# Mixer and feed-forward kernel: diagonals and loads of x placed in other slices of the opening

## The reference

```
low = x
for two levels:
    l = dwconv(low, h_filter)[:, ::2];  h = dwconv(low, g_filter)[:, ::2]     # 4 taps per channel, stride 2
    highs.append(h);  low = l
low = linear_attention(low, 16 heads)          # q = k = elu(x)+1, v = x, kv summed over the whole sequence
for the two levels, backwards:
    low = dwconv(repeat2(low), h_synth) + dwconv(repeat2(h), g_synth)
a = layer_norm(x + low, gamma, beta)
x1 = layernorm(x + a)
y = (silu(x1 @ wg.T) * (x1 @ wu.T)) @ wd.T     # 1536 hidden, integer weights times 1/127
out = layernorm(x1 + y)
```

## Time and profile before

| | us |
|---|---|
| median of 3 runs | 1210.11 |
| lowest and highest of them | 1209.3, 1210.5 |
| the profiled execution, its own time | 1209.61 |
| its span, from the first to the last instruction | 1207.8 |
| TensorE busy in the span | 1173.7 (97%) |
| VectorE busy | 973.1 (81%) |
| ScalarE busy | 672.6 (56%) |
| POOL busy | 303.1 (25%) |

### The profile page before, as it was taken

One profiled execution on the slowest core, in us unless ns is written; L12 is line 12 of the kernel. 1 busy time (PEld: TensorE's weight loads), 2 busy tenths in 40 slices (PEclk: granted clock), 3 DMA queues, 4 the chain that ended last, 5 costly groups with the idle time before them and its releaser, 6 DMA issues.

```text
span 1207.8 us, 19489 instructions
## 1 busy us (share of the span) xinstructions
PE 1173.7 (97%) x6456; PEld 604.4 (50%) x6456; DVE 973.1 (81%) x1951; ACT 672.6 (56%) x1403; POOL 303.1 (25%) x730
## 2 busy tenths in 40 slices
PE   6888999999999999999999999999999999999997
PEld 5567644445445544445445444444445444454443
DVE  7797999998999989997997779867997689845331
ACT  6954744677346854576346644666346644565342
POOL 0014322152314313152213412142304313131101
PEclk9998999999999999999999999999999999999999
DMA  7886520222212310222102310211111310110000
GB/s 263 271 201 142 184 61 19 106 97 89 71 44 79 128 40 18 98 83 74 36 27 97 98 35 18 105 62 53 35 58 64 106 35 11 42 55 1 3 34 35
DMA packets 52301, 92.96 MB, mean 77 GB/s; under 512 B 9072, under 2 KB 28784, under 8 KB 51312
## 3 DMA queue, kind: packets, MB, share of 16 engines
q1 hardware_dynamic: 50480, 87.10, 21.9%
q0 software_dynamic: 1728, 4.72, 2.2%
HBM read 67.09 MB, written 25.19 MB: 76 GB/s over the span
## 4 chain that ended last, share of the span: by engine, by line
PE 81%; DVE 6%; ACT 5%; issue 4%; POOL 3%; DMA 1%; SPq 0%; POOLq 0%; ACTq 0%; DVEq 0%
PE ps_up L679 12%; PE ps_up L680 12%; PE ps_gate L679 12%; PE ps_gate L680 12%; PE ps_down L698 12%; PE ps_down L697 12%; PE ps_x L622 2%; PE ps_y L640 2%; DVE l L1286 1%; PE ps_x L601 1%; POOL rs L1216 1%; PE ps_down L864 1%; DVE h L1286 1%; ACT x_hi L1136 1%; DVE hid L1286 1%
## 5 line engine op out<-in xcount | busy, mean ns | idle before, releaser
L697 PE MATMUL ps_down<-w,hid 128*128 128x512 f16 x768 | 291.4, 379 | 1.2 <-DVE hid L1672 1.0
L698 PE MATMUL ps_down<-w,hid 128*128 128x512 f16 x768 | 291.3, 379 | 0.0
L679 PE MATMUL ps_up<-x_hi,w 128*128 128x512 f16 x760 | 288.4, 379 | 0.9 <-DVE h_f L1685 0.9
L679 PE MATMUL ps_gate<-x_hi,w 128*128 128x512 f16 x760 | 288.4, 379 | 0.5 <-ACT h_f L1160 0.5
L680 PE MATMUL ps_gate<-x_lo,w 128*128 128x512 f16 x760 | 288.3, 379 | 0.0
L680 PE MATMUL ps_up<-x_lo,w 128*128 128x512 f16 x760 | 288.2, 379 | 0.0
L1160 ACT ACTIVATE h_f<-ps_gate 128x512 f32<-128x512 f32 x192 | 113.9, 593 | 205.6 <-PE ps_gate L680 204.6
L1685 DVE SCALAR_TENSOR_TENSOR h_f<-ps_up,h_f 128x512 f32<-128x512 f32 x192 | 130.9, 685 | 110.1 <-PE ps_up L680 97.7
L1152 ACT ACTIVATE hid<-h_f 128x512 f16<-128x512 f32 x192 | 119.7, 623 | 42.0 <-DVE h_f L1685 42.0
L1672 DVE TENSOR_TENSOR hid<-h_f,hid 128x512 f16<-128x512 f32 x192 | 130.9, 682 | 1.9 <-ACT hid L1152 1.0
L679 PEld LDWEIGHTS ps_up<-x_hi,w 128*128 128x128 f16 x760 | 74.2, 98 | 91.5 <-DVE h_f L1685 1.8
(11 more groups left out here) (260 smaller groups left out, 1688.0 us busy)
## 6 DMA issues: line engine op xcount, KB each, us to landing
xt<-x_tok SPq DMA_DIRECT2D x64, 256.0 KB, 2.7
out<-x SPq DMA_DIRECT2D x64, 256.0 KB, 2.0
xb<-x_chan SPq DMA_DIRECT2D x7, 2060.0 KB, 7.7
xa<-x_chan SPq DMA_DIRECT2D x20, 515.0 KB, 5.0
w<-weights POOLq DMA_DIRECT2D x12, 384.0 KB, 9.9
att<-den SPq DMA_DIRECT2D x32, 129.5 KB, 2.7
xa<-x_phase SPq DMA_DIRECT2D x8, 515.0 KB, 6.4
q_in<-q_scratch SPq DMA_DIRECT2D x7, 518.0 KB, 4.5
```

What stands on the lines that cost most here:

```text
L679: pe.matmul(ps_gu[k % 2][g][:, :], w, x1_hi[:, b, c, :], start=(c == 0), stop=False)
L697: pe.matmul(ps_d[t % 2][:, :], h_hi[:, k, t * P:(t + 1) * P], w, start=(k == 0), stop=False)
L698: mm = pe.matmul(ps_d[t % 2][:, :], h_lo[:, k, t * P:(t + 1) * P], w, start=False, stop=(k == NH - 1))
```

## The change

Three things are moved; no work is added or removed.

1. The 28 diagonals were made in slices 1, 2 and 3 (10, 10 and 8), each time behind the turn copies. They are now made in six portions of a table DIAGS: 4 in slice 0 ahead of pro_l1, 5 in slice 0 between the band_firsts and out1_copy(0, 2), then 3, 3, 3 and 10 in slices 1, 2, 3 and 4 behind the turn copies.
2. The unheld loads of x: slice 0 was loaded in the order chunk 3, 0, 1, 2 and is loaded as 0, 1, 3, 2; slice 1 was loaded as 3, 0, 1, 2 and is loaded as 0, 1, 3, 2.
3. The loads of xb, chunks 2 and 3, were issued at the end of loop steps 1 and 2. Both are now issued at the end of step 3.

```
+DIAGS = ((0, 4), (4, 5), (9, 3), (12, 3), (15, 3), (18, 10))
...
-            load_pro(0, 3)
             for c in range(2):
                 sp.dma_start(xb[:, c, :], x_chan[:, 0, c, :]).then_inc(ld_x0[c], 16)
+            load_pro(0, 3)
             load_pro(0, 2)
-            for c in (3, 0, 1, 2):
+            for c in (0, 1, 3, 2):
                 load_pro(1, c)
...
-                if a in (1, 2):
-                    sp.dma_start(xb[:, a + 1, :], x_chan[:, 0, a + 1, :]).then_inc(ld_xb0, 16)
+                if a == PER_BATCH - 1:
+                    for c in (2, 3):
+                        sp.dma_start(xb[:, c, :], x_chan[:, 0, c, :]).then_inc(ld_xb0, 16)
...
             for a in range(NPRO):
                 if a == 0:
+                    pro_diags(*DIAGS[0])
                     pro_l1(a, 0)
                     pro_l1(a, 1)
                 else:
...
                 pro_band_firsts(a, 1)
+                if a == 0:
+                    act.wait_ge(coef_ready, 6)
+                    pro_diags(*DIAGS[1])
                 pro_out1_copy(a, 2)
...
-                if a == 1:
-                    act.wait_ge(coef_ready, 6)
-                if 1 <= a <= 3:
-                    pro_diags(10 * (a - 1), 10)
+                if a > 0:
+                    pro_diags(*DIAGS[a + 1])
                 pro_out2_copy(a, 3)
                 pro_out2_copy(a, 2)
```

## The result

| | before | after |
|---|---|---|
| median of 11 runs, us | 1209.3 | 1212.27 |
| lowest and highest, us | 1207.8, 1210.5 | 1209.65, 1214.11 |
| profiled execution, its own time, us | 1209.61 | 1213.84 |
| its span, us | 1207.8 | 1212.0 |

The ratio is 1.0023 (95%: 1.0015 to 1.003), 2.8 us (3.0 by the medians), where 1.1 us was forecast. The forecast of 1211.2 us was counted from a median of 1210.11; from the 1209.3 of these eleven runs the same +1.1 would be 1210.4. The profiled execution is one of the slower ones of after: it lost 4.2 us in its span. The runs also lie further apart than before, 4.5 us against 2.7, and the fastest of the eleven is the one with the highest mean granted clock (0.996, against 0.993 to 0.995 in the others).

What follows compares the result with a forecast made beforehand. The opening was taken as bound by TensorE's conv2 behind ScalarE's waits, the main loop by a full TensorE. +2.1 - 0.1 - 0.5 - 1.3 + 0.9 = +1.1 us gave a median of 1211.2, range 1208.2 to 1213.5.

Steps and rivals of the forecast that it cites:

- rival (2): One more fall of TensorE's clock, at the wait for keys_sum ahead of the turns: +3.1, 1213.2 us, chance 0.18.
- Start, +2.1: Slice 0: later first product and diagonals delay slice 1's first VectorE tap, S(1), by +2.1 us, bounds +1.7 and +3.3.
- second of the two cases: Slice 0: TensorE's clock rises at the same time as before, conv1(0, 3) ends at 13.0, S(1) is 20.8: +1.7.
- The early low1_taps: Slice 0: VectorE's low1_taps could end 1 us sooner, but this gains nothing.
- Rival (4): The change's start costs nothing because the clock is up before TensorE begins: 1209.1 us, chance 0.05.
- Diagonals, -0.1 and -0.5: Slices 1 and 2: ScalarE is relieved of 2.0 us each, but only TensorE's lead counts: -0.1 and -0.5 us.
- Rival (1): ScalarE alone is the bound, so each relief counts in full: -6.5, 1203.6 us, chance 0.08.
- Slice 3, -1.3 from the clock: Slice 3: TensorE's clock, low from 50 to 54 us, does not fall there: -1.3 us, bounds -1.3 and 0.
- the store term: Slice 4: h2 store lands late behind two xb loads: +0.9 us if slice 3 is short, 0 if long.
- Slice 4, +0.9: Slice 4: the moved xb loads delay slice 3's h2 store and the denominators: +0.9 us, bounds 0 and +2.3.
- a shift is passed on one to one: From slice 4 on, a shift of its first VectorE tap, S(4), passes in full through denominators, att and weight loads.
- rival (3): At pro_s(2, 1), the late slow stretch shrinks, saving 1 to 3.0 us: 1208.2 to 1210.2 us, chance 0.22.

Runs made afterwards that it cites:

- e1: Kernel before with only the new order of the first loads of x; 1211.93 us, ratio 1.0019.
- e9: Kernel before with TensorE's idle waits filled by transposes, plus only the new order of the x loads; 1208.59 us, ratio 0.9987.
- e2: Kernel before with only the diagonals placed as in the change; 1208.99 us, ratio 1.0001.
- e10: Kernel before with TensorE's idle waits filled by transposes, plus only the new places of the diagonals; 1207.58 us, ratio 0.998.
- e5: Kernel after with five warming products on zeros on TensorE ahead of conv1(0, 3); 1211.1 us, ratio 1.0011.
- e6: Kernel after with TensorE's idle waits in the opening filled by unread transposes of ident; 1208.22 us, ratio 0.9989.
- e7: Kernel before with TensorE's idle waits in the opening filled by unread transposes of ident; 1206.02 us, ratio 0.9976.
- e3: Kernel before with only the two loads of xb moved to step 3; 1210.45 us, ratio 1.0003.
- e11: Kernel before with TensorE's idle waits filled by transposes, plus only the two xb loads moved to step 3; 1206.46 us, ratio 0.997.
- e12: e6 with the two xb loads directly behind the store of h2 in step 4 instead of ahead of it; 1208.54 us, ratio 0.9988.
- e8: Kernel before with new x order, diagonals 4, 0, 3, 3, 6, 12, five warming products and transposes filling TensorE's waits; 1205.27 us, ratio 0.9968.
- e4: Kernel after with nine warming products on zeros on TensorE ahead of conv1(0, 3); 1212.59 us, ratio 1.0031.

## Why the prediction came out as it did

The forecast put 1211.2 us and "the same" first; measured is 1212.27 and a slowdown just past the 0.2% that a measurement can tell, a case that had a chance of 0.16. The direction and the largest term were right. That the two times lie only 1.1 us apart is in part luck: the median of before came out 0.8 us lower than the one I counted from, and the added time was +2.8 to +3.0 us, not +1.1. Nearest is the sum of rival (2), +3.1.

**Start, +2.1: right, +2.02.** The first product came at 9.40 us (9.5 was said), and it went as in the second of the two cases: conv1(0, 3) was done at 13.1, the five diagonals let ScalarE go at 17.05, conv2(0, 2) ran until 19.7. That case alone had been priced at +1.7; the two between them gave 2.1, and over seven kernels the move is 2.4. (Two slips of the working: it says that S(1) follows the copy by 1.35 us but adds 1.46, where 1.33 was measured; and the stated range ends at 1213.5 us, below the 1213.8 of its own bounds.) Both halves are shown alone: the order by e1 (+1.39 at S(1)) and e9 (+1.73), the diagonals by e2 (+0.85) and e10 (+1.43), the half speed of TensorE's first products by e5 (-1.73). The early low1_taps gained nothing: VectorE began them at 8.07 and then idled 2.72 us behind the copy for TensorE. Rival (4) falls with this.

**Diagonals, -0.1 and -0.5: right in mechanism.** ScalarE's relief turned into idle time ended by ps_down, as was said; it is there with the clock up too (1.80 us in slice 1 of e6). The ten diagonals of slice 4 cost nothing up to the denominators (S(4) + 8.72 in e2 and e10). Rival (1), ScalarE alone as the bound, fell by that. The bound itself is seen only with the clock up: e6 has 12.28 and 12.27 us in slices 1 and 2, e7 12.40 and 13.58, so -0.1 and -1.3. The second is more than predicted, and it is not the diagonals' own: alone they give 0.04 there (e10), with the xb load gone from ahead of the store of slice 1 they give the rest. That load I had put at nothing, because it had time to drain; the store landed 0.6 to 1.5 us sooner without it.

**Slice 3, -1.3 from the clock: the step that failed.** The loss did go from slice 3 (12.28 us), and came back in slices 1 and 2 (13.91 and 13.92), 1.6 us over e6's each. That is the mechanism of rival (2), though with the fall of slice 3 gone and two others in its place: the three slices together came to +0.71 us, where my terms say -1.9 and rival (2) +1.0. I treated the fall as fixed to a slice of a kernel, gone or not. It moves with the execution: slice 1 took 12.38 us before and 13.89 in e3, whose clock fell ahead of the first instruction in which the two differ. The Trainium skill's page "TensorE: Matmul & The Clock Gate" (Part 1: The HAM clock gate) says that the gate's monitor runs freely and that the moment of change varies with it; these two traces agree, and I had cited it against the rivals but not against my own term. If the other executions of before have such falls too, the median already contains them, and the gain of 1.3 was hardly to be had. Without it, and with the store term at 0 that then goes with it, the prediction's own terms give +1.5 us; the pair with the clock held up gave 1.6 to 2.2, the pair as it is 2.8. The last of these differences, 0.6 to 1.2 us, would be the falls of one kernel being more or longer than those of the other; that was not counted over many executions and stays an inference.

**Slice 4, +0.9: mis-sized, and then not passed on.** At the denominators it was +2.14 us (e3 +1.73, e6 +1.70), within the bounds of 0 and 2.3 but near the upper. With the two loads ahead of it the store landed 6.1 to 6.5 us behind its issue (e3, e11, after, e6), with them behind it 4.8 (e12). What failed is "a shift is passed on one to one": in e12 the denominators came 2.0 us sooner than in e6, and the seventh weight load landed no sooner. A delay of the denominators counts only as far as it delays the landing of the weights.

**Late stretch, rival (3):** it stayed (6.84 us for twenty products, 7.31 before). In e3 it did not come (4.55), nor in any filled kernel. It too moves with the execution.

**The path behind the denominators.** POOL's wait between its two blocks of weight loads was 17.12 us after and 15.20 before; over the kernels it is between 14.80 (e8) and 17.46 us (e4). It is the time until the seventh load has landed. The seven land one behind another within 11.2 to 12.1 us of the first in every kernel; what differs is how long the first takes from its issue, 6.65 us before and 8.95 after. The prediction passed a shift of S(4) on through the issue of the weight loads one to one, which leaves this out. What stays open is what stood ahead of the first in the queue in each kernel, and why it took 8.0 and 8.7 us in e7 and e9, where the xb loads are as before: no run was made to explain it.

## What to carry to other kernels

Ask of every engine's idle time which engine ended it, and order the first loads for the engine that has the longest and slowest start; a load that comes early for an engine that then waits for another gains nothing. Where TensorE idles a little again and again and its clock falls by chance, don't forecast one fall away: price the falls as an average that both kernels carry, or fill the waits and compare the kernels so. And a load in a full queue delayed what waited behind it wherever it was put (the stores of slices 1 and 3, the att load): move it to where the queue is empty or nobody waits. Follow such a delay to the landing of the loads that end the stretch, not to their issue.

## What the runs showed of the hardware

**Throwaway products pay.** Eighty-eight transposes in waits of TensorE of 1.2 to 3.1 us brought 3.5 us (1209.53 to 1206.02), with the granted clock at 1.00 from 20 to 110 us. **The clock column does not show the start.** The window of after over conv1(0, 3):

```profile
9.40:13.00 3.60, 3.60 (x20) 2.81 (x21) 2.83 (x5) 0.00 (x0) 0.00 (x0) 1.00 0.99 374
```

It says 1.00, but the first seven of these products took 1.95 us where seven of the same shape took 1.10 in e5, behind a TensorE already at work. At the start the speed must be read from durations. **A wait does not fix a fall.** TensorE waited 2.31 us ahead of the transposes in slice 1 and 2.29 in slice 3, with a fall behind the second alone; across the kernels slice 1 took 12.3 or 13.9 us. **POOL's loads come in blocks.** Seven weight loads are issued, and the eighth 0.39 or 0.40 us behind the landing of the seventh, in fourteen of fourteen traces, with no wait in the code.
